# A decoder layer on one core: the first two attentions project five head groups ahead instead of three

## The reference, cut to what matters

```python
q, k, v = (split_heads(lora_linear(x, w, a, b)) for ...)      # first attention
scores = q @ k.T / sqrt(32); scores = where(causal, scores, -inf)
x = layernorm(x + lora_linear(softmax(scores) @ v, wo, ao, bo))
h = ln1(x + mha(x, x, x))                                     # second attention, "self"
h = ln2(h + mha(h, ctx, ctx))                                 # third attention, "cross"
h = ln3(h + relu(h @ fc1_w + fc1_b) @ fc2_w + fc2_b)
x = layernorm(x + h)
x = layernorm(x + quantized_ffn(x))                           # last three lines: not touched
```

## Time and profile before

| what | value |
|---|---|
| median of three runs | 3752.34 us |
| the profiled execution's own time | 3748.11 us |
| its span, first to last instruction | 3746.2 us |
| mean granted TensorE clock | 0.948 of full speed |
| TensorE busy (PE) | 3276.4 us, 87% |
| VectorE busy (DVE) | 2740.9 us, 73% |
| ScalarE busy (ACT) | 2109.1 us, 56% |

### The profile page before, as it was taken

The page is one execution under the profiler, slowest core; times in us unless marked ns, Lnnn a source line. Parts: engine busy times, 40 slices in busy tenths (PEclk is TensorE's granted clock), DMA queues, the critical chain, the costliest instruction groups (busy, mean ns, idle before and its releaser), DMA issues. The chain is left out here.

```text
span 3746.2 us, 90438 instructions
## 1 busy us (share of the span) xinstructions
PE 3276.4 (87%) x36576; PEld 2536.9 (68%) x36576; DVE 2740.9 (73%) x4907; ACT 2109.1 (56%) x4664; POOL 789.4 (21%) x802
## 2 busy tenths in 40 slices
PE   7999999599999569999999999999816999999995
PEld 4888888377777447777777777777714565656562
DVE  4777777477777658888888888888853666666666
ACT  2665656266666427777777777776643444444442
POOL 0111111034444401121211112112211121212121
PEclk9999999799999779999999999999858999999998
DMA  3333333234433243333333333332232000000000
GB/s 100 92 107 97 107 98 90 95 108 119 118 107 110 79 125 100 93 98 96 92 99 91 95 99 95 102 95 77 66 143 94 18 29 23 29 23 29 27 20 17
DMA packets 246148, 309.33 MB, mean 83 GB/s; under 512 B 108932, under 2 KB 166276, under 8 KB 245095
## 3 DMA queue, kind: packets, MB, share of 16 engines
q1 hardware_dynamic: 245734, 303.54, 27.1%
HBM read 212.45 MB, written 90.64 MB: 81 GB/s over the span
## 5 line engine op out<-in xcount | busy, mean ns | idle before, releaser
L745 ACT ACTIVATE cross_p_hi<-cross_ps 125x448 f16<-125x448 f32 x768 | 418.1, 544 | 335.3 <-PE cross_ps L700 324.7
L808 DVE TENSOR_TENSOR cross_p_lo<-cross_ps,cross_p_hi 125x448 f16<-125x448 f32 x768 | 475.4, 619 | 145.5 <-ACT cross_ps L746 145.0
L801 DVE TENSOR_REDUCE cross_mx<-cross_ps 128x1 f32<-128x750 f32 x512 | 475.4, 929 | 35.8 <-PE cross_ps L666 35.2
L746 ACT ACTIVATE cross_ps<-cross_ps 125x448 f32<-125x448 f32 x768 | 417.8, 544 | 0.0
L666 PE MATMUL cross_ps<-cross_qk_stack 96*128 96x375 f16 x1024 | 256.1, 332 | 98.4 <-DVE cross_mx L801 95.2
L1254 PE MATMUL ffn_ps_f<-ffn_xt,ffn_f_hi 128*128 128x256 f16 x1792 | 298.0, 274 | 10.4 <-ACT ffn_ht L1326 5.3
L591 PE MATMUL cross_ps<-cross_w_hi,cross_ct 128*125 128x128 f16 x3072 | 297.2, 221 | 0.0
L700 PE MATMUL cross_ps<-cross_qk_stack 97*125 97x224 f16 x1536 | 290.5, 272 | 2.8 <-DMA cross_qk_stack<-cross_mrow 2.8
L719 PE MATMUL cross_ps<-cross_vs,cross_p_hi 125*128 125x65 f16 x3072 | 287.6, 193 | 2.9 <-ACT cross_o_raw L752 2.1
L591 PEld LDWEIGHTS cross_ps<-cross_w_hi,cross_ct 128*125 128x125 f16 x3072 | 285.2, 138 | 0.3
L1270 PE MATMUL ffn_ps_c<-ffn_f_hi,ffn_ht 128*128 128x512 f16 x896 | 284.1, 379 | 0.0
(11 more groups left out here) (260 smaller groups left out, 9548.4 us busy)
## 6 DMA issues: line engine op xcount, KB each, us to landing
cross_spill<-cross_proj SPq DMA_DIRECT2D x64, 487.0 KB, 3.0
cross_c_rows<-ctx SPq DMA_DIRECT2D x48, 500.0 KB
cross_qk_stack<-cross_spill SPq DMA_DIRECT2D x128, 187.5 KB, 3.6
cross_qk_stack<-cross_spill SPq DMA_DIRECT2D x64, 243.5 KB, 3.1
causal_spill<-causal_proj SPq DMA_DIRECT2D x64, 224.0 KB, 2.0
causal_qk_stack<-causal_spill SPq DMA_DIRECT2D x256, 56.0 KB, 2.0
self_spill<-self_proj SPq DMA_DIRECT2D x64, 224.0 KB, 2.0
self_qk_stack<-self_spill SPq DMA_DIRECT2D x256, 56.0 KB, 2.0
```

Of the source, the lines that this page charges most:

```text
L745: act.activation(p_hi[:, n % 4, :], scores, ACT.Exp, scale=EXP_SCALE)
L746: act.activation(scores, scores, ACT.Exp, scale=EXP_SCALE).then_inc(exp_done, 1)
L801: dve.tensor_reduce(mx[:, g, t, h:h + 1], ps_qk[:, :, 0:KT // 2], AX.XY, ALU.max).then_inc(max_done, 1)
L808: dve.tensor_tensor(p_lo[:, n % 4, :], ps_st[0:KC, st_bank(g, n), 0:2 * T], p_hi[:, n % 4, :], ALU.subtract).then_inc(lo_done, 1)
```

## The change

The rules of `step` are replaced by a table that writes the order out. For `causal` and `self` it places the same events in the same order inside a step, apart from SyncE's loads and stores, but for groups that lie further ahead: projections five steps ahead (before three), maxima three (two), the row two (one), scores as before.

```diff
+    "self": (("E1 S1 residual load qka qkb spill row stack M0 V0 S2 M1 V1 E0 S3 v0a v0b M2 V2 S0 M3 V3",
+                 "E1 S1 qka qkb spill row stack M0 V0 S2 norm M1 V1 E0 S3 apply v0a v0b M2 V2 S0 M3 V3",
+                 "E1 S1 qka qkb spill row stack M0 V0 S2 v0a v0b M1 V1 E0 S3 x0 M2 V2 S0 x1 M3 V3",
...
+               (5, 3, 2, 1)),
...
+        RING = 4 if cross else 6 if causal else 6
+        qk_stack = sb("qk_stack", [97, RING, GH, T + KT], F16)
...
-        vs = sb("vs", [KC, G, NCH, GH, VW], F16)
-        mx = sb("mx", [P, G, 2, GH], F32)
+        vs = sb("vs", [KC, RING, NCH, GH, VW], F16)
+        mx = sb("mx", [P, RING, 2, GH], F32)
...
-        STACK_DMAS = 5
+        STACK_DMAS = 4
...
+        def place(b, g):
+
+            return (G * b.first + g) % RING
...
         def inputs_split(k):
 
-
-            return job_index[kv_name, k, 0] if cross or k < 2 else job_index[LAST_V, k - 1, 3]
+            return max(job_index[kind, k, 0] for kind in IN_JOBS)
...
-                    sp.dma_start(qk_stack[0:HD, g], heads[:, :, T:2 * T + KT]).then_inc(stacked[g % 2], 16)
-                    for r, q_at in ((HD, T), (2 * HD, 0)):
-                        sp.dma_start(qs[r:r + HD, g], heads[:, :, q_at:q_at + T]).then_inc(stacked[g % 2], 16)
-                        sp.dma_start(ks[r:r + HD, g], heads[:, :, 2 * T + KT:]).then_inc(stacked[g % 2], 16)
+                    at = place(b, g)
+                    for w in range(2):
+                        sp.dma_start(qk_stack[(1 + w) * HD:(2 + w) * HD, at],
+                                     heads[:, :, w * (T + KT):(w + 1) * (T + KT)]).then_inc(stacked[g % 2], 16)
+                    sp.dma_start(qs[0:HD, at], heads[:, :, T + KT:2 * T + KT]).then_inc(stacked[g % 2], 16)
+                    sp.dma_start(ks[0:HD, at], heads[:, :, T:T + KT]).then_inc(stacked[g % 2], 16)
```

More of the change, by code:

```diff
@@ L299, in loads, with unit @@
                     yield "load c", Batch(b), 0, n
+            def unit(u):
+                for kind in UNIT_JOBS:
+                    yield from halves_of(kind, Batch(u // G), u % G)
+                    if kind == LAST_K:
+                        yield "spill", Batch(u // G), u % G, 0
+                yield "stack", Batch(u // G), u % G, 0
             yield from loads(0)
@@ L303, in prologue @@
             yield from loads(1)
[L305 to L311, removed]
             yield from unit(0)
             yield from unit(1)
[L316 to L320, removed]
+            work = list(inputs(1))
+            for u in range(2, JOBS_AHEAD):
+                work += list(unit(u))
+            maxima = [("max", Batch(0), g, t) for g in range(MAX_AHEAD) for t in range(QTILES)]
             for n, m in enumerate(maxima):
@@ L323, in prologue @@
                 yield m
-            yield "row", Batch(0), 0, 0
+            for g in range(ROW_AHEAD):
+                yield "row", Batch(0), g, 0
             for n in range(AHEAD):
@@ L328, in step @@
         def step(b, g):
[L331 to L349, removed]
@@ L350, in step @@
-            if b.i is not None or b.first > 0:
-                jobs += [(kind, b + -1, 0, 0) for kind in OUT_JOBS.get(g, [])]
-            if (b + 2).exists(NB):
-                jobs += [(kind, b + 2, 0, 0) for kind in IN_JOBS.get(g, [])]
-            maxima = [("max", b2, g2, t) for t in range(QTILES)] if b2.exists(NB) else []
-            if g == NORM_STEP and (b.i is not None or b.first > 0):
-                items.append(("norm", b + -1, 0, 0))
-            stored = b + (-2 if has_wo else -1)
@@ L358, in step @@
-            if g == STORE_STEP and (b.i is not None or stored.first >= 0):
-                items.append(("store", stored, 0, 0))
-            slots, last = [[] for _ in range(PAIRS)], [[] for _ in range(PAIRS)]
-            groups = []
-            for job in jobs:
-                if job[0] in ("spill", "stack"):
-                    groups[-1].append(job)
-                else:
-                    groups.append([job])
-            for n, group in enumerate(groups):
-                slots[n * PAIRS // len(groups)] += group
@@ L651, in perform @@
                                 out = ps_proj[:, bank, at:at + nt]
-                                if biases is not None and 0 in halves:
+                                if biases is not None and 0 in parts:
                                     pe.matmul(out, b_pair[:, col:col + P], ones[:, 0:nt], start=True, stop=False)
@@ L655, in perform @@
                                                      lambda j, c: rows[:, b.par, j, c, t0:t0 + nt],
[L656 removed]
+                                                     first=biases is None, halves=parts)
                     if 1 in halves:
```

138 lines of the change are left out of this document (77 added, 61 removed), and 15 rows, old and new, of the table ORDERS.

## The result

The changed kernel took 3790.33 us (median; 3785.28 to 3794.47) against 3753.06 us (3751.57 to 3754.25): a ratio of 1.0099 with a 95% interval of 1.0081 to 1.0116, so 37 us slower. The forecast was 3806 us, the range 3778 to 3836.

The account below looks back on a forecast made before the run. TensorE, busiest at 87% of the span, was taken as the limit in `causal` and `self`. Terms 37.5 + 12.6 + 22.0 - 5.2 + 1.5 - 11 - 3 = +54.4 us on 3752.3 gave 3806, range 3778 to 3836.

Parts of the forecast that it names:

- The wait that comes: Step 3 of `causal` and `self`: TensorE's projection waits for VectorE's low part of `x1`, 14 times each, 37.5 us.
- The 14.4 of mrow at nothing: Step 1 of `self`: removing 14.4 us of mrow waits gains nothing, as TensorE then waits for VectorE's maximum instead.
- The waits that go: TensorE's waits for the stack in both phases and mrow in `causal`, 12.5 us together, go for a gain of 11.
- The clock: The new waits bring eight more falls of TensorE's clock to 1.2 GHz, 1.57 us each, 12.6 us slower.
- rival A: The new wait is paid but brings no falls, perhaps takes present ones along: 3793 down to 3778; chance 0.16.
- The ends of a phase: Prologues of `causal` and `self` grow by 22.0 us; steps without projections at the phase ends give back 5.2.
- The memset: VectorE's first memset grows with the ring from 16 to 24 rows and TensorE's first transposes wait: 1.5 us, once.
- `cross`: An earlier stack takes away 2.9 us of waits in `cross`; a gain of 3 taken with its prologue.
- A clock below 1.00 in `causal`: A sign the forecast was right: the profile after would show a mean clock under 1.00 in `causal`, before at 1.00.
- C: Rival: VectorE's low part of `x1` is ready when the projection begins, so the new wait is covered: 3725; chance 0.04.
- D: Rival: the new wait is small and step 1 stays as costed: 3757, within 0.2%; chance 0.05.
- B: Rival: nearly every new wait brings a clock fall, 28 instead of 8: 3837; chance 0.13.

Follow-up runs that it names:

- Experiment 4: The changed kernel with the old leads 3, 2, 1, 1 and rings of four, transposes at the end of step 0 directly before their projection: 3797.19 us, 1.0117.
- experiment 5: The changed kernel with its leads kept, transposes moved to the end of step 0, rows loaded a batch earlier: 3761.35 us, 1.0017 to the kernel before.
- 11: The changed kernel with the norm, its application and the store of `self` moved late, transposes still in step 2: 3750.82 us, 0.9997 to the kernel before.
- experiment 2: The changed kernel with the old leads 3, 2, 1, 1 and a ring of four, the rest of the change kept: 3755.32 us, 1.0008.
- experiment 6: The changed kernel with transposes in step 0, rows loaded earlier, norm and application late, store of `self` moved: 3713.93 us (0.9890), again 3709.95 us (0.9882).
- 7: The changed kernel with leads 3, 2, 1, 1, rings of four, transposes in step 2, loads behind the stack, norm and `self` store late: 3726.64 us, 0.9927.
- experiment 8: The changed kernel with leads 4, 2, 1, 1, transposes in step 0, norm and `self` store late, loads ahead of the projections: 3791.14 us, 1.0096.
- 10: The changed kernel with leads 4, 2, 1, 1, transposes in step 0, norm and `self` store late, loads behind the stack: 3736.32 us, 0.9955.

## Why the prediction was right

The direction, the cause and the size of the main term came out. The sum of 54.4 is to be held against 46.4 in the profile, and against 37 between the medians. It is nearer than its terms: the clock was put some 11 us too high and `cross` with what follows it 10 us too low, and these two cancel, which is luck. In the profile 37.3 + 19.7 - 3.9 + 1.9 + 0.7 (between `causal` and `self`) + 7.0 - 16.4 = 46.3. Term by term:

- **The wait that comes.** 37.5 forecast, 14.9 + 22.4 = 37.3 found, 14 times in each phase and 1.60 us each in `self` where 1.57 was said. Experiment 4 makes the wait without the lead, 5 removes it and gets 31 us back, 11 keeps it: this cause is shown.
- **The 14.4 of mrow at nothing.** Found over the twelve batches: 12.5 less before mrow, 11.2 more before `self_mx`. The trade itself is not the lead's: in experiment 2, with the old leads, step 1 has lost its wait for mrow already and waits for `self_mx` instead, and what the lead adds is the loss of the waits in step 0. The reading of the 14.4 as about 1 us in every batch was rough, too: one wait of 3.50 is in it, so the others average 0.78. Experiments 6, 7 and 11 show the reason that was given: with VectorE's norm out of the way the second wait goes, and only then does the lead earn what its transfers promised. By the Trainium skill's rule in "DMA: Bandwidth & Descriptors", "Rules for kernel authors" (issue early, wait late), the 14.4 was to be gained; the trace agrees with it in experiment 6 against 7 (26.1 us in the twelve batches of both phases), and disagrees in experiment 5 against 2 (5.2 us). Here it held only where the transfer's wait was the one that ended last.
- **The waits that go.** 11 forecast. In `self` the stack's 6.7 went to 0.4; in `causal` the lists had 4.1 + 1.7. Without the twelve waits for `xt` (19.2 and 12.6) the windows of twelve batches are 11.6 and 3.2 us shorter, and the seven groups before them (from the second evacuation of group 0 to that of group 7), less their own four waits, 2.3 shorter in `causal` (64.44 to 64.50, with waits of 2.35) and 0.7 longer in `self` (59.54 to 63.47, with 3.2): 16.4. The lists of waits over the twelve batches, without `xt`, explain most of it. In `causal` 4.7 us for transfers went and 1.1 for VectorE came, which makes 3.6 beside the 3.2. In `self` 18.7 went and 12.1 came, which makes 6.6 of the 11.6; 1.6 more comes from 3.4 us less at half clock, and for some 3 us I know no row.
- **The clock, the step that failed.** 12.6 us for eight more falls: the twelve batches of `self` have nine stretches in both traces, one of them of double length before (at the wait of 3.50), and a mean of 0.96 in both. The seven groups before them have three where there was one. That is 3.4 us more at half clock in the steps, about 1.5 us. The end of `self`, which is counted below, has some 11 us more of it. Falls came behind five of the fourteen new waits; in the twelve batches three of the nine did, and the other six stand behind step 1. Had this term been nothing, the sum would be 41.8. It was rival A's condition that the new wait brings no falls or takes present ones along, and the measured 3790 lies inside A's 3793 to 3778, at the lower edge of the forecast's own 3790 to 3822. What failed is the step from the wait to the number of falls: the count was added to that of the kernel before, as if the old falls stayed. Against experiment 2, which has the old leads and five stretches, the change has four more, experiment 4 has five more, and experiment 5 is back at six, by one trace of each; but the rest of the change had taken four away. The unit price of 1.57 was not contradicted: for the same matmuls TensorE is busy for 379.87 us with 34.0 us at half clock (before), 376.17 with 30.6 (after) and 364.22 with none (experiment 6), which makes 1.57 and 1.33 for each 3.4 us. The Trainium skill, "TensorE: Matmul & The Clock Gate", "What's actually happening", has it that waits as short as these leave the clock alone. The trace disagrees again, with a clock of 0.51 behind a wait of 1.60, though only five of fourteen such waits had one behind them.
- **The ends of a phase.** Prologues 22.0 forecast, 11.0 + 8.7 = 19.7 found; first scores of `causal` at 84.62 ("after 82"). The first row's transfer alone waits 4.20 instead of 2.54. Ends: 5.2 less forecast, 0.5 + 3.4 = 3.9 found; in `causal` one step that lost its projections went from 8.39 to 7.39, but the next from 7.88 to 8.42; why it grew is not shown. In the working, two groups at 3.65 are 7.3 and not 7.6.
- **The memset.** 1.5 forecast, 4.54 - 3.04 = 1.50 found; the first projection is 1.9 later, since the longer memset also began 0.37 later.
- **`cross`.** A gain of 3 forecast, a loss of 4.8 found, and what followed `cross` is 2.2 longer. The stack's 2.9 went, as forecast, but the waits for `cross_mx` grew from 95.2 to 100.5, a wait of 1.9 for the rows of the context is new, and there are thirteen short stretches at half clock where there were twelve. (The wait of 2.8 for the first mrow is in both kernels.) Experiment 2 and all the others have the same loss behind `self`, 7.0 us or more, so it belongs to the change; with one trace of the kernel before its size is uncertain.
- **A sign that failed.** A clock below 1.00 in `causal` was to be seen. It is 1.00 in the twelve batches, as before.

By rivals: C (the wait is covered) and D (it is small) are out by the list of waits; B (28 falls) is out by the clock. A is the one that the clock bears out, and its range holds the measured time. That a lead can be right and not help was in none of them as a mechanism of its own; it is what experiments 5 and 6 found.

## What to carry to other kernels

When a lead is lengthened, look for every other input of the step that is moved, here the transposed rows: the distance from its producer shrinks by as much as the distance to the consumer grows. A transfer's wait is worth removing only where no engine is late right behind it, so take the late engine's work out of the way first and then lengthen the lead; here the late norm alone gave 27 us (0.9927), the two together, with the transposes moved out of the way, 43 (0.9886), and the lead alone lost 37. Small loads that are issued ahead of a chain of dependent transfers on one queue cost 53 us in one kernel (experiment 8 against 10) and nothing that shows in another (the change), so their place is worth a trial whenever a lead is changed.

## What the runs showed of the hardware

- A memset over one partition takes time by its length: 3584 elements took 3.04 us, 5376 took 4.54, that is 0.85 and 0.84 ns per element.
- The clock of `self`, at 0.96 in both kernels, is 1.00 over the twelve batches of experiment 6: with the waits of step 1 and of `xt` removed, the falls are gone too, and with them the 1.57 us that each had cost.
- With experiment 8's waits of up to 3.3 us in `causal` the clock fell there too (0.97); with waits of 1.05 in front of `causal_xt`'s projection, once per batch, it stayed at 1.00 (the kernel after). In `self` of experiment 7 it stayed at 1.00 with waits of up to 1.7 for mrow, while single waits of 1.03 and 1.60 had a fall behind them in the kernels before and after. So the length of a wait alone does not tell whether the clock falls.
